# Gates of a cell by blocks of plain fp32 products, one block of 32 rows for each chunk of channels

## The reference, cut to what matters

```python
def xattn(q, k, v, ifgate_w, ifgate_b, outnorm_w):        # q = layernorm(x); k = v = ctx
    gate_in = concat([q, k, v], -1)                       # 16 x 256 tokens, 3 x 256 channels
    pre = gate_in @ ifgate_w.T + ifgate_b                 # 16 columns: 8 heads, input and forget gate
    pre = 15 * tanh(pre / 15)
    i_pre, f_pre = pre[..., :8], pre[..., 8:]
    h = mlstm_parallel(q, k, v, i_pre, f_pre)             # scores weighed by exp of sums of the gates
    return h * rsqrt(mean(h * h)) * (1 + outnorm_w)       # per head of 32 channels
def ffn(x):                                               # ternary weights, hidden width 1024
    h = silu(x @ w1.T * s1) * (x @ w2.T * s2)
    h = gelu(h @ h1.T * s_h1)
    h = gelu(h @ h2.T * s_h2)
    return h @ w3.T * s3
x = x + xattn(layernorm(x), ctx, ctx, ...)                # all in float32
x = x + ffn(layernorm(x))
```

## Time and profile before

| | us |
|---|---|
| median of 3 runs | 785.65 (785.62 to 785.66) |
| the profiled execution's own time | 785.57 |
| its span, first to last instruction | 783.7 |
| mean granted clock of TensorE in the span | 0.995 |

### The profile page before, as it was taken

The page is one execution under the profiler, slowest core; times in us unless marked ns, Lnnn a source line. Parts: engine busy times, 40 slices in busy tenths (PEclk is TensorE's granted clock), DMA queues, the critical chain, the costliest instruction groups (busy, mean ns, idle before and its releaser), DMA issues.

```text
span 783.7 us, 14916 instructions
## 1 busy us (share of the span) xinstructions
PE 772.8 (99%) x6162; PEld 640.4 (82%) x6162; DVE 555.1 (71%) x1311; ACT 378.6 (48%) x555; POOL 50.3 (6%) x61
## 2 busy tenths in 40 slices
PE   8999999999999999999999999999999999999997
PEld 7878788887888878878888878888788887888886
DVE  5887867587765869569685887758695694955544
ACT  3246644455464643556345564546445562445331
POOL 2300020000200001000200002000020000000000
PEclk9989999999999999999999999999999999999999
DMA  9924000500023001220004100140012100540540
GB/s 343 353 79 158 28 29 28 189 1 29 30 79 138 27 10 48 110 81 28 31 28 148 41 29 29 36 182 1 28 56 109 54 1 3 180 143 20 169 135 28
DMA packets 14902, 63.42 MB, mean 81 GB/s; under 512 B 2048, under 2 KB 3440, under 8 KB 12016
## 3 DMA queue, kind: packets, MB, share of 16 engines
q1 hardware_dynamic: 13248, 50.34, 18.5%
q0 software_dynamic: 1296, 11.53, 3.7%
q10 hardware_dynamic: 288, 0.57, 0.2%
HBM read 53.94 MB, written 8.50 MB: 80 GB/s over the span
## 4 chain that ended last, share of the span: by engine, by line
PE 82%; DVE 14%; ACT 2%; issue 2%; POOL 0%; DVEq 0%; POOLq 0%; ACTq 0%
PE ps_f L1412 24%; PE ps_f L1413 23%; DVE decay L873 9%; PE ps_f L1386 8%; PE ps_f L1389 8%; PE ps_f L1447 4%; PE ps_f L1448 4%; PE ps_a L1329 2%; DVE decay L889 2%; PE ps_a L1306 2%; PE ps_a L1200 1%; PE ps_a L1357 1%; PE ps_f L1532 1%; PE ps_a L1279 1%; PE ps_a L1272 1%
## 5 line engine op out<-in xcount | busy, mean ns | idle before, releaser
L1412 PE MATMUL ps_f<-h_hi,wgt 128*128 128x512 f32 x1024 | 404.6, 395 | 0.0
L1413 PE MATMUL ps_f<-h_lo,wgt 128*128 128x512 f32 x1024 | 399.4, 390 | 0.0
L1412 PEld LDWEIGHTS ps_f<-h_hi,wgt 128*128 128x128 f32 x1024 | 192.2, 188 | 41.4 <-issue 0.3
L1413 PEld LDWEIGHTS ps_f<-h_lo,wgt 128*128 128x128 f32 x1024 | 192.3, 188 | 38.1
L1029 DVE TENSOR_TENSOR h_lo<-work,h_hi 128x512 fp32r<-128x512 f32 x128 | 86.5, 690 | 110.0 <-ACT h_hi L666 108.9
L661 ACT ACTIVATE work<-ps_f,scl 128x512 f32<-128x512 f32 x128 | 87.4, 683 | 153.0 <-PE ps_f L1413 152.9
L1386 PE MATMUL ps_f<-h_hi,wgt 128*128 128x512 f32 x256 | 101.4, 396 | 0.2 <-ACT h_hi L638 0.2
L1389 PE MATMUL ps_f<-h_lo,wgt 128*128 128x512 f32 x256 | 100.6, 393 | 0.3 <-DVE h_lo L1006 0.3
L648 ACT ACTIVATE work<-ps_f,scl 128x512 f32<-128x512 f32 x64 | 44.1, 688 | 92.8 <-PE ps_f L1389 92.8
L666 ACT ACTIVATE h_hi<-work 128x512 fp32r<-128x512 f32 x128 | 81.0, 633 | 4.1
L1020 DVE SCALAR_TENSOR_TENSOR work<-ps_f,scl,work 128x512 f32<-128x512 f32 x64 | 48.1, 751 | 47.7 <-ACT work L648 47.7
(11 more groups left out here) (184 smaller groups left out, 705.0 us busy)
## 6 DMA issues: line engine op xcount, KB each, us to landing
decay<-m_rows SPq DMA_DIRECT2D x14, 1024.0 KB, 5.9
decay<-w_cols SPq DMA_DIRECT2D x22, 512.0 KB, 4.4
wgt<-w_cols POOLq DMA_DIRECT2D x5, 1024.0 KB, 14.5
v_aug<-ctx_tok SPq DMA_DIRECT2D x8, 528.0 KB, 3.7
wgt<-w_cols POOLq DMA_DIRECT2D x2, 2048.0 KB, 14.5
x_kept<-xs SPq DMA_DIRECT2D x8, 512.0 KB, 2.6
xs<-x SPq DMA_DIRECT2D x7, 512.0 KB, 3.6
ctxT<-ctx_t SPq DMA_DIRECT2D x7, 512.0 KB, 3.8
```

What stands on the lines that cost most here:

```text
L1412: pe.matmul(ps_f[:, bank], w, moving(h_hi[layer][:, k], as_is), start=(k == 0), stop=False)
L1413: last = pe.matmul(ps_f[:, bank], w, moving(h_lo[layer][:, k], as_is), start=False, stop=(k == KH - 1))
```

## The change

Pairs 2 to 7 make their gates from `ctxT` and `zT` as they are, in plain fp32. Each of the four chunks (two of the normed input, two of the keys and values, which share their weights' sum) has its own block of 32 rows of `gate_out`: 16 rows for one gate, 16 for the other. That is one product for each chunk and batch, 8 in all, with a stationary tile of 32 columns. ScalarE copies all 128 rows (`take_gate_parts`), and behind group 3 of the layer TensorE adds up the four blocks with one product by `gather`, a matrix of ones and zeros, into rows 0 to 47 of `gate_out` (`gather_gates`). The tanh reads from there. The copies to high halves, the subtractions to low halves, VectorE's addition and the wait at L665 go; `block_gate_weights` takes the place of `split_gate_weights` in the head.

```diff
@@ GpSimd, head
-                pool.memset(gw_split[:].bitcast(F32), 0.0).then_inc(s_gw_clear, 1)
...
+            def block_gate_weights():
+
+                pool.memset(gw_blocks[:], 0.0).then_inc(s_gw_clear, 1)
+                pool.memset(gather[:], 0.0).then_inc(s_gw_clear, 1)
+                pool.wait_ge(s_ident, 5)
+                pool.tensor_tensor(gather_half, ident[:, 0:P // 2], ident[:, P // 2:P], ALU.add).then_inc(s_gw_blocks, 1)
+                pool.wait_ge(s_gw_clear, 2)
+                dst = gw_blocks[:, :, HEADS:].rearrange("p c (k e) -> p c k e", k=2)[:, :, :, 0:HEADS]
+                src = gw_in.rearrange("p c (k g) -> p c k g", k=2)
+                pool.tensor_copy(dst[:, 0:CH], src[:, 0:CH]).then_inc(s_gw_blocks, 1)
+                pool.tensor_tensor(dst[:, CH:2 * CH], src[:, CH:2 * CH], src[:, 2 * CH:3 * CH], ALU.add).then_inc(s_gw_blocks, 1)
+                pool.wait_ge(s_gw_blocks, 1)
+                to = gather[:].rearrange("p (k x) -> p k x", k=2)[:, :, 0:W * HEADS]
+                of = gather_half.rearrange("p (n k x) -> p n k x", n=2, k=2)
+                pool.tensor_tensor(to, of[:, 0], of[:, 1], ALU.add).then_inc(s_gw_blocks, 1)
@@ GpSimd, loop
-                if g < PAIRS:
-                    split_keys_low(g)
-                    split_normed_low(g)
@@ ScalarE
-                act.activation(keys_hi, ctxT(j), ACT.Copy).then_inc(s_keys_hi, 1)
...
-                act.activation(normed_hi, source, ACT.Copy).then_inc(s_zhi, 1)
-
-            def take_gate_low(j):
+
+            def take_gate_parts(j):
                 act.wait_ge(s_gate, j + 1)
-                act.activation(gate_low, gate_out[ROW_LOW:SPLIT_COLS], ACT.Copy).then_inc(s_gate_low, 1)
+                act.activation(gate_parts, gate_out, ACT.Copy).then_inc(s_gate_parts, 1)
...
-                if layer == 1 and m == 4 and isinstance(i, int) and i + 2 < PAIRS:
-                    act.wait_ge(s_gate, i + 3)
@@ VectorE
-            def add_gate_low(j):
-                dve.wait_ge(s_gate_low, j - W + 1)
-                dve.tensor_tensor(gate_sum, gate_out[0:GATE_COLS], gate_low, ALU.add).then_inc(s_gate_sum, 1)
@@ TensorE
                 if isinstance(j, int) and 0 < j < PAIRS - 1:
 
-                    pe.wait_ge(s_zhi, j)
+                    pe.wait_ge(s_zTe, j + 2)
@@ TensorE, gates(j)
-                pe.wait_ge(s_gw_split, 4)
-                pe.wait_ge(s_keys_lo, j - W + 1)
+                pe.wait_ge(s_gw_blocks, 4)
+                pe.wait_ge(s_ctxT[j % 2], 16 * (j // 2) + 16)
                 pe.wait_ge(s_zTe, j + 1)
...
                 for b in range(W):
...
+                    at = slice(HEADS * (1 - b), HEADS * (1 - b) + GATE_BLOCK)
+                    for n in range(2 * CH):
+                        source = ctxT(j) if n >= CH else zT(j)
+                        last = pe.matmul(gate_out[n * GATE_BLOCK:(n + 1) * GATE_BLOCK], gw_blocks[:, n, at],
+                                         source[:, n % CH, b * SEQ:(b + 1) * SEQ], start=(b == 0), stop=(b == W - 1))
                 last.then_inc(s_gate, 1)
+
+            def gather_gates(j):
+
+                pe.wait_ge(s_gate_parts, j - W + 1)
+                pe.matmul(gate_out[0:GATE_COLS], gather[:, 0:GATE_COLS], gate_parts, start=True, stop=True)\
+                  .then_inc(s_gate_sum, 1)
...
                     if g_stage and m == 2:
                         gates(g)
+                    if g_stage and m == 3:
+                        gather_gates(g)
```

More of the change, by code:

```diff
@@ L56 @@
 GATE_COLS = ROW_FLOOR + BH
-ROW_LOW = 64
-SPLIT_COLS = ROW_LOW + GATE_COLS
-SPLIT_WIDTH = SPLIT_COLS + HEADS
+GATE_BLOCK = 2 * W * HEADS
 COMPARED_BEFORE_LAST = 6
@@ L89, in build @@
         z2_hi, z2_lo = h_hi[1][:, 0:CH], h_lo[1][:, 0:CH]
-        keys_hi, keys_lo = h_hi[0][:, 4:4 + CH], h_lo[0][:, 4:4 + CH]
-        normed_hi, normed_lo = h_hi[0][:, 6:6 + CH], h_lo[0][:, 6:6 + CH]
         decay = sb("decay", [P, BH * SEQ])
@@ L113, in build @@
         gw_in = num[:, 512:512 + 3 * CH * 2 * HEADS].rearrange("p (c g) -> p c g", g=2 * HEADS)
-        gw = num[:, 608:608 + 2 * CH * 2 * HEADS].rearrange("p (c g) -> p c g", g=2 * HEADS)
         z2 = num[:, 0:Q * DIM].rearrange("p (q d) -> p q d", q=Q)
@@ L123, in build @@
         head_mask = sb("head_mask", [P, CH, ROWGRP, DV])
-        gw_split = sb("gw_split", [P, 2 * CH, SPLIT_WIDTH], F32R)
+        gw_blocks = sb("gw_blocks", [P, 2 * CH, HEADS + GATE_BLOCK])
+        gather = sb("gather", [P, 2 * ROW_FLOOR])
+        gather_half = num[:, 800:800 + P // 2]
         scl = sb("scl", [P, 4, KH])
@@ L151, in build @@
         s_gw_clear = sem("s_gw_clear")
-        s_gw_whole = sem("s_gw_whole")
-        s_gw_split = sem("s_gw_split")
+        s_gw_blocks = sem("s_gw_blocks")
         s_lead = sem("s_lead")
@@ L185, in build @@
         s_zTe = sem("s_zTe")
[L186 to L189, removed]
         s_gate = sem("s_gate")
-        s_gate_low = sem("s_gate_low")
+        s_gate_parts = sem("s_gate_parts")
         s_gate_sum = sem("s_gate_sum")
@@ L250, in plain @@
             return j < W
-        gate_low = decay[0:GATE_COLS, Q * DIM:Q * DIM + SEQ]
-        gate_sum = decay[0:GATE_COLS, Q * DIM + SEQ:Q * DIM + 2 * SEQ]
+        gate_parts = decay[:, Q * DIM:Q * DIM + SEQ]
         f_row = state[0:BH, 0:SEQ]
@@ L472, in place_gate_weights @@
                 pool.tensor_tensor(dst[:, CH:2 * CH], src[:, CH:2 * CH], src[:, 2 * CH:3 * CH], ALU.add).then_inc(s_gw_plain, 1)
-            def split_gate_weights():
-                pool.memset(gw_split[:].bitcast(F32), 0.0).then_inc(s_gw_clear, 1)
[L477 to L489, removed]
+            def block_gate_weights():
[12 more added lines that the diff above has]
+                pool.tensor_tensor(to, of[:, 0], of[:, 1], ALU.add).then_inc(s_gw_blocks, 1)
             def weigh_keys(j):
@@ L499, in weigh_keys @@
                 last.then_inc(s_kwt, 1)
[L501 to L507, removed]
             pool.memset(ident[:], 0.0).then_inc(s_ident, 1)
@@ L529, in _ @@
             load_weights((4, 5, 6, 7, 8))
-            split_gate_weights()
+            block_gate_weights()
             pool.wait_ge(s_gain, 16)
@@ L533, in _ @@
             for i in range(PAIRS):
-                j, g = i + 1, i + 2
+                j = i + 1
                 if j < PAIRS:
                     weigh_keys(j)
-                if g < PAIRS:
-                    split_keys_low(g)
-                    split_normed_low(g)
             def general_path(i):
@@ L581, in soft_cap @@
                     act.wait_ge(s_gate_sum, j - W + 1)
-                act.activation(rows[0:GATE_COLS], gate_out[0:GATE_COLS] if plain(j) else gate_sum, ACT.Tanh, bias=gb[:], scale=1.0 / CAP).then_inc(s_gact, 1)
+                act.activation(rows[0:GATE_COLS], gate_out[0:GATE_COLS], ACT.Tanh, bias=gb[:], scale=1.0 / CAP).then_inc(s_gact, 1)
             def softplus(j):
@@ L618, in take_near @@
                 if first(j):
-                    act.wait_ge(s_gw_split, 4)
+                    act.wait_ge(s_gw_blocks, 4)
                     act.wait_ge(s_pv, TILES)
@@ L685, in batch @@
                 if g_stage:
-                    split_keys(g)
                     take_zT(g)
@@ L690, in batch @@
                     if g_stage and m == 2:
-                        take_gate_low(g)
+                        take_gate_parts(g)
                     if g_stage and m == 3:
@@ L915, in first_num @@
                 if b == 0:
-                    dve.wait_ge(s_gw_split, 4)
+                    dve.wait_ge(s_gw_blocks, 4)
                 dve.wait_ge(s_far, 1)
@@ L1123, in batch @@
                         norm_2_apply(j, xs[j % 2])
-                    if g_stage and m == 2:
-                        add_gate_low(g)
                     if g_stage and m == 3:
@@ L1260, in gates @@
             def gates(j):
-                pe.wait_ge(s_gw_split, 4)
-                pe.wait_ge(s_keys_lo, j - W + 1)
+                pe.wait_ge(s_gw_blocks, 4)
+                pe.wait_ge(s_ctxT[j % 2], 16 * (j // 2) + 16)
                 pe.wait_ge(s_zTe, j + 1)
                 pe.wait_ge(s_num, j)
-                to = gate_out[0:SPLIT_COLS]
                 for b in range(W):
[L1269 to L1280, removed]
+                    at = slice(HEADS * (1 - b), HEADS * (1 - b) + GATE_BLOCK)
[3 more added lines that the diff above has]
+                                         source[:, n % CH, b * SEQ:(b + 1) * SEQ], start=(b == 0), stop=(b == W - 1))
                 last.then_inc(s_gate, 1)
+            def gather_gates(j):
+                pe.wait_ge(s_gate_parts, j - W + 1)
+                pe.matmul(gate_out[0:GATE_COLS], gather[:, 0:GATE_COLS], gate_parts, start=True, stop=True)\
+                  .then_inc(s_gate_sum, 1)
             def turn_rows(j):
```

## The result

| | us |
|---|---|
| kernel before, median of 19 runs | 785.38 (784.33 to 785.66) |
| kernel after, median of 19 runs | 786.33 (785.14 to 786.83) |
| ratio after to before, 95% interval | 1.0014 (1.0007 to 1.0020) |
| the profiled execution of after, its span | 786.25, 784.5 |
| one pass of the loop, mean of five: before, after | 92.17, 92.34 |

The account below looks back on a forecast made before the run. TensorE's issue time was taken to bound the kernel: per pair 1.24 + 0.58 = 1.82 us added against 1.88 removed, over six pairs 0.4 us less, from 785.57 to 785.2 us. Range 783.4 to 787.6; forecast no change (within 0.2%), chance 0.66.

Parts of the forecast that it names:

- TensorE alone sets the time in this stretch: Second hidden layer, where the gates stand: TensorE's issue is paid in full, other engines cost nothing until TensorE waits.
- What is removed, 1.88 us a pair: Gates of pairs 2 to 7: sixteen TensorE products of 256 columns go, 1.88 us per pair including the product behind.
- The strips, 1.24 us, four at once: Gates' eight fp32 products of 32 output rows: four rounds of 0.222 (0.89) plus 0.35 fixed, 1.24 us per pair.
- Rival 3: Gates' strips don't run together over 256 columns: 790.5 us if two run at once, 801.2 if one; chance 0.08.
- three-strip efficiency: Gates' strips: 2.38 times measured for three column strips, applied to four, makes rounds 1.12 us and the kernel 786.6.
- The adding product, 0.58 us with ends 0.44 and 0.63: Product summing the gates' four blocks: 0.443 streaming, 0.08 for leaving, 0 to 0.09 for entry; 0.58 us per pair.
- the strips' fixed 0.35: Gates' packed block: fixed cost on top of its rounds, taken between 0.20 (two edges alone) and the scores' 0.40 us.
- The sum: Gates, per pair: 1.24 + 0.58 = 1.82 against 1.88 us, 0.06 less; six pairs 0.4 us, giving 785.2.
- The upper end of the strips: Gates' strips if long rows pack only threefold: 3.55/3.1 + 0.40, given as 1.54 us per pair.
- Rival 4: Lone adding product not pipelined with its neighbours: a record's whole 0.38 exposed, about +0.38 us a pair, 787.5; chance 0.07.
- Covers: Work costed at nothing: ScalarE's parts copy about 3 us ahead of need, tanh about 5 us earlier, head weights 2 us.
- rival 2: Freed VectorE and ScalarE time shortens TensorE's waits at the scores: 6 x 0.18 = 1.1 us, 784.1; chance 0.05.

Follow-up runs that it names:

- experiment 4: Kernel after without the adding product, the tanh reading one of the four parts of the gates' sum: 781.81 us, ratio 0.9958; a pass 0.79 us less.
- experiment 5: Kernel after with ScalarE's two copies and GpSimd's two subtractions put back in their old places, results unused: 785.90 us, ratio 1.0013.
- experiment 6: Kernel after with the gates' eight fp32 products unpacked, 48 output rows each, summed in place, without parts copy or adding product: 797.11 us.
- experiments 1 to 3: Kernel after with the adding product's stationary tile padded from 48 to 128, 80, 64 columns: 784.72 us (128); passes 92.07, 91.96, 92.31 us.
- experiments 9 and 10: Kernel after with 128-column adding product, and kernel before, each with attention's values blocks joined and the state's reading moved later: 780.76 and 780.38 us.
- joined128: Kernel after with 128-column adding product, attention's values blocks joined and the state's reading moved later: 780.76 us, ratio 0.9946.

## Why the prediction was off, step by step

- *TensorE alone sets the time in this stretch.* Right: experiment 4 gives back what the start-to-start reading of the adding product says (0.79 for 0.77), and experiment 5 puts the other engines' work back for nothing.
- *What is removed, 1.88 us a pair.* Right by the rows, and not touched by anything since.
- *The strips, 1.24 us, four at once.* Measured 1.21 (rounds of 0.24, 0.22, 0.22, and 0.31 to the next product, with 0.09 and 0.11 at the edges). Rival 3 falls: without packing the same products take 3.79 (experiment 6). The Trainium skill's three-strip efficiency, which would have made the rounds 1.12 us, is not what this trace shows: the last round starts 0.68 us behind the first, 0.227 a round where a single record takes 0.222.
- *The adding product, 0.58 us with ends 0.44 and 0.63.* This is the step that failed: it measured 0.77, outside its ends. I took it for a full-width product, because its neighbour form in the trace was a transpose, and left open only "0 to 0.09" for entering. But a stationary tile of 48 columns is a packed one. It pays the entry (0.09), the exit (0.11), and a third thing that I had counted in the strips' fixed 0.35 and not here: the last record isn't overlapped by the next product (0.56 for two records instead of 0.443, 0.12). Rows that show a part of it were there. The head's products of 48 columns are of this form: from the start of the 8 records at 11.77 to the next product at 13.63 are 1.86 us for 8 steps, 0.08 more than 8 x 0.222, which lies in that last step, and I used only the steps inside. They don't show the entry. The Trainium skill, page "TensorEngine Tiling (Array Packing)", section "Tiling Modes", lists 128x64 as a form of its own, two tiles wide; experiments 1 to 3 agree, with the step between 64 and 80 columns. I had cited its rule of the drain for the strips and not asked it of the other product that the change adds.
- *The sum.* With 0.77 in place of 0.58, and 1.21 in place of 1.24, a pair costs 1.98 against 1.88; six pairs, +0.6 us, 786.2 from the profiled 785.57. The profiled execution took 786.25. The passes say +0.17 each. Over all of passes 1 to 5, distance by distance, the blocks make +0.11 of it (1.22 + 0.77 against 1.88). The other 0.06 lies in no block: away from the blocks the main products follow each other after 0.2281 us on average instead of 0.2279, some 272 times a pass. Why stays open. That the time fell within the range and within 0.2% says little for the sum, since the miss of the adding product alone (6 x 0.19 = 1.1 us) is smaller than either margin. The upper end of the strips was divided by 3.1 where the text says threefold (1.58 instead of 1.54); nothing hangs on it.
- *Rival 4* had the cause nearest: the lone product not overlapped with its neighbours. It was priced at a record's whole length, 0.38 more; it was 0.19 more.
- *Covers.* All held. ScalarE copied the parts at 212.40, 3.5 us ahead of the adding product at 215.93; the tanh began at 217.29 instead of 223.14; neither the adding product nor the turn of the rows waited for it. The freed time (rival 2) reached TensorE nowhere.

## What to carry to other kernels

Price a TensorE block from the start of the main product ahead to the second main product behind, less the two steps, and do so for each form of block that an edit adds, also for a single product: here a block of tiles of 64 columns or fewer cost some 0.3 us on top of its streaming. Where a product is narrow and stands alone, pad its stationary tile with zeros past 64 columns (0.77 became 0.45 us); where there are several packed blocks, join them, and look what the work that stood between them had covered, and at the whole time as well as at a pass (experiments 9 and 10).

## What the runs showed of the hardware

The two groups of times, some 1.1 us apart, come from the head. The stretches of 39 to 46 us of two executions, first the kernel after (the later group; columns: stretch, its length, busy us and instructions of PE, PEld, DVE, ACT, POOL, granted clock, DMA share, GB/s), then experiment 5 (the earlier group):

```profile
39.00:44.00 5.00, 5.00 (x18) 3.35 (x18) 3.44 (x11) 2.05 (x5) 0.00 (x0) 0.50 0.35 141
44.00:46.00 2.00, 2.00 (x8) 1.05 (x7) 1.83 (x5) 1.11 (x1) 0.00 (x0) 0.69 0.00 0
```

```profile
39.00:44.00 5.00, 5.00 (x30) 3.13 (x28) 4.03 (x14) 2.82 (x5) 0.00 (x0) 1.00 0.29 116
44.00:46.00 2.00, 2.00 (x20) 2.00 (x19) 1.97 (x2) 1.96 (x4) 0.00 (x0) 1.00 0.00 0
```

In the first the granted clock is at its lower level (0.50, 1.2 GHz) for these 5 us, behind a stretch of small products with 33 columns; in the second it stays at 2.4 GHz. Eight of the twelve traces have the lower clock in this stretch (0.50, or 0.67 in experiments 1 and 2), and their first scores begin at 64.55 to 64.61; in the other four they begin at 63.17 to 63.62. What counts is not the whole stretch but the end of the 33-column products, for which VectorE waits. The order of time of VectorE, the kernel after and then experiment 5:

```profile
39.87 0.43 DVE L878 TENSOR_TENSOR num<-ps_f,state 128x264 f32<-128x264 f32 x1 [0.73 <-PE ps_f L1292]
```

```profile
38.94 0.43 DVE L908 TENSOR_TENSOR num<-ps_f,state 128x264 f32<-128x264 f32 x1 [0.17 <-PE ps_f L1322]
```

That is 0.93 of the 0.96 us between their first scores (64.58 and 63.62). In these two traces the products themselves also began 0.37 apart; in `joined128` they began at 35.07 as in experiment 5 (35.05), and VectorE's operation still at 39.89. From there to the main products at 55 us the chain that ended last runs almost wholly over VectorE, so TensorE's slow work of 40 to 46 us costs nothing more. Executions of both groups occur for one and the same kernel: the kernel after has mean clocks of 0.993 to 0.997 in the later group and 0.997 to 1.0 in the earlier one, though only one execution of each kernel was traced. Why the clock falls in some only isn't shown. A change worth 1 us is as large as this, which is why the passes were compared.

The other is how long a small VectorE operation can stand beside GpSimd: 2.05 and 1.90 us instead of 0.2 for 32 elements a partition, each ending with a GpSimd subtraction (experiment 5). The Trainium skill, page "SBUF — State Buffer", section "SBUF: two separate sides", says that the two engines share a pair of ports as an exclusive lock, also for a VectorE operation with two inputs from SBUF against a GpSimd one that reads SBUF; the rows agree. It cost nothing here because VectorE had the time to lose.
